# S4 convolution and int4 SwiGLU on one core: later resolvent sums, an earlier load of the shifted kernel, and moved work and loads in the last group

## What is computed

```
x = x + s4(layernorm(x)) + ffn(layernorm(x))

s4:  denom = g[:, None] - Lambda[None, :]            # g: 1024 roots of unity
     cauchy = lambda v: (v[None, :] / denom).sum(-1)
     at_roots = c * (k00 - k01 * (1.0 / (1.0 + k11)) * k10)
     K = ifft(at_roots, L).real                      # L = 1024
     y = irfft(rfft(u, n=2L) * rfft(K, n=2L))[..., :L] + D[0] * u

ffn: Wg, Wu (2752 x 1024), Wd (1024 x 2752): int4, (w - zero) * scale in groups of 64
     h = silu(xn @ Wg.T) * (xn @ Wu.T)
     return h @ Wd.T
```

## Time and profile before

| | us |
|---|---|
| three runs | 1406.25, 1406.70, 1408.76 (median 1406.7) |
| the profiled execution's own time | 1407.06 |
| its span, first to last instruction | 1405.2 |
| TensorE busy (matmuls) | 1318.3 (94%) |
| VectorE busy | 968.1 (69%) |
| GpSimd busy | 682.4 (49%) |
| ScalarE busy | 463.0 (33%) |
| mean granted TensorE clock | 0.976 of 2.4 GHz |

### The profile page before, as it was taken

The page is one execution under the profiler, slowest core; times in us unless marked ns, Lnnn a source line. Parts: engine busy times, 40 slices in busy tenths (PEclk is TensorE's granted clock), DMA queues, the critical chain, the costliest instruction groups (busy, mean ns, idle before and its releaser), DMA issues.

```text
span 1405.2 us, 17059 instructions
## 1 busy us (share of the span) xinstructions
PE 1318.3 (94%) x6302; PEld 625.5 (45%) x6302; DVE 968.1 (69%) x1038; ACT 463.0 (33%) x825; POOL 682.4 (49%) x483
## 2 busy tenths in 40 slices
PE   3688899999999999999999999879999999999998
PEld 2544344344444444444444444334454444444444
DVE  7965799899899989999898988433253433332432
ACT  5744545444544444445454543310000000000000
POOL 6772777777777777879797886610000000000000
PEclk7799999999999999999999999989999999999999
DMA  8111545454555445455545454998345335336331
GB/s 308 32 46 38 166 146 154 126 182 139 161 143 168 133 135 154 147 158 151 163 141 175 128 153 140 381 373 311 113 153 176 98 129 202 99 114 218 98 97 60
DMA packets 165168, 218.09 MB, mean 155 GB/s; under 512 B 42204, under 2 KB 122718, under 8 KB 163166
## 3 DMA queue, kind: packets, MB, share of 16 engines
q1 hardware_dynamic: 164222, 202.79, 46.1%
q10 hardware_dynamic: 864, 14.22, 2.5%
HBM read 139.64 MB, written 77.34 MB: 154 GB/s over the span
## 4 chain that ended last, share of the span: by engine, by line
PE 51%; DVE 2%; SPq 2%; DMA 1%; issue 1%; POOL 1%; ACT 0%; ACTq 0%; DVEq 0%
PE px L1443 15%; PE px L1357 10%; PE pz L1443 8%; PE pv L1470 6%; PE pz L1357 5%; PE py L1443 4%; PE py L1357 2%; DMA kshift<-kpad 1%; SPq L596 1%; DVE wf L1555 1%; DMA w_d<-ds 0%; SPq L600 0%; DVE wf L1527 0%; PE pv L1484 0%; DVE hf L1653 0%
## 5 line engine op out<-in xcount | busy, mean ns | idle before, releaser
L1357 PE MATMUL px<-xo,wo 128*128 128x512 f16 x2016 | 467.4, 386 | 19.2 <-ACT u L986 10.8
L1357 PEld LDWEIGHTS px<-xo,wo 128*128 128x128 f16 x2016 | 198.4, 99 | 264.0 <-issue 28.6
L686 POOL TENSOR_TENSOR wo<-wf,wo 128x512 f16<-128x512 f32 x147 | 239.4, 1638 | 74.9 <-ACT wo L932 74.9
L705 POOL TENSOR_TENSOR hs<-hf,hs 128x512 f16<-128x512 f32 x154 | 211.0, 1376 | 114.9 <-ACT hs L967 114.7
L1443 PE MATMUL px<-wd,hr 128*128 128x512 f16 x1056 | 232.3, 379 | 0.0
L1357 PE MATMUL pz<-xo,wo 128*128 128x512 f16 x1008 | 231.3, 379 | 0.1
L1443 PEld LDWEIGHTS px<-wd,hr 128*128 128x128 f16 x1056 | 102.2, 98 | 118.7
L1357 PEld LDWEIGHTS pz<-xo,wo 128*128 128x128 f16 x1008 | 98.6, 98 | 118.6 <-issue 0.8
L1971 DVE SCALAR_TENSOR_TENSOR acc<-px,acc 128x512 f32<-128x512 f32 x32 | 22.1, 690 | 154.1 <-PE px L1443 126.4
L967 ACT ACTIVATE hs<-hf 128x512 f16<-128x512 f32 x154 | 94.4, 621 | 91.3 <-DVE hf L1619 43.9
L932 ACT ACTIVATE wo<-wf 128x512 f16<-128x512 f32 x147 | 91.4, 623 | 90.0 <-DVE wf L1528 80.7
(11 more groups left out here) (229 smaller groups left out, 1415.0 us busy)
## 6 DMA issues: line engine op xcount, KB each, us to landing
h_d<-hs SPq DMA_DIRECT2D x154, 256.0 KB, 2.4
hr<-h_d SPq DMA_DIRECT2D x56, 704.0 KB, 4.3
w_d<-ds SPq DMA_DIRECT2D x73, 256.0 KB, 2.3
wd<-w_d ACTq DMA_DIRECT2D x4, 2816.0 KB, 15.2
sz<-in_sz_gate SPq DMA_DIRECT2D x21, 512.0 KB, 5.0
sz<-in_sz_up SPq DMA_DIRECT2D x21, 512.0 KB, 4.9
sz<-in_sz_down SPq DMA_DIRECT2D x20, 512.0 KB, 5.3
xc_d<-xo SPq DMA_DIRECT2D x8, 1024.0 KB, 7.7
```

The source lines that it names most:

```text
L686: pool.tensor_tensor(w_dest(t, j, 1), w_place_of(j), w_dest(t, j, 0), ALU.subtract).then_inc(wlo_done, 1)
L705: pool.tensor_tensor(hs[:, j, :, 1, :], h_place_of(p, j), hs[:, j, :, 0, :], ALU.subtract)\
L1357: done = pe.matmul(bank[:, :], wo[t % 2][:, j, wp, k * P:(k + 1) * P], xo[p][:, j, xp, k, :], start=(j in (0, 3) and k == 0 and wp == 0 an ...
```

## The change

1. **Resolvent blocks.** TensorE multiplies block m in unit 8 + 2m, not 7 + 2m. The steps behind it move two units back on VectorE (roots 24, columns 26, rows 28, scale 31) and on TensorE (25, 27, 30). `angle` gets two buffers, and a load waits for the block before the last.
2. **kshift and flip.** `kshift` has a place of its own (over small tables that are done with) and is loaded at the end of group 8, beside unit 32 and after; `flip` is loaded at the start.
3. **Words and scales** have semaphores apart: nibbles wait for words alone.
4. **The short piece's high nibbles** are made by ScalarE (`tail_nibble`), twice 96 rows; VectorE waits for them.
5. **Loads and stores at the change of phase.** The first `acc` are loaded by ScalarE's queue, ahead of `wd3` and `wd4`, once the last `h_second` is done; on SyncE's queue `hr` of product 4 goes ahead of the last seven stores of `h`, and `wd6` behind `hr` of product 5.

The core of the diff (`slab_in` is `words_in` and `scales_in` in the functions left out too, and `angle[m % 2]` stands for `angle`):

```diff
 def slab_arrived(m):
-    return 32 * (m // 2 + 1) + 32 * (m % 2) * ((m >= 63) + (m >= 65))
+    return 16 * (m // 2 + 1) + 16 * (m % 2) * ((m >= 63) + (m >= 65))
...
-        kshift = at("kshift", [P, 2, SB], f32, W0 + 24 * K1)
-        flip = at("flip", [P, P], f32, X0 + 55 * K1)
...
-        angle = small("angle", [P, 2, P])
+        angle = [at(f"angle{i}", [P, 2, P], f32, H0 + i * K1) for i in range(2)]
+        flip = small("flip", [P, P])
+        kshift = at("kshift", [P, 2, SB], f32, place[0])
...
             def load_angle(m):
-                if m > 0:
-                    sp.wait_ge(resolvent_done, m)
+                if m == 0:
+                    sp.wait_ge(xt_done, 56)
+                if m >= 2:
+                    sp.wait_ge(resolvent_done, m - 1)
...
+                if g == 8:
+                    sp.wait_ge(kpad_out, 48)
+                    for n in range(2):
+                        sp.dma_start(kshift[:, n, :], bass.AP(kpad.tensor, n * (P + L // 2) + 1, [[1, P], [1, SB]]))\
+                            .then_inc(kshift_in, 16)
...
             store_h(NG, 0, S4)
-            sp.dma_start(flip[:, :], flip_d).then_inc(flip_in, 16)
-            sp.wait_ge(kpad_out, 48)
-            sp.wait_ge(deq_done, slab_tail(1, 1) + 1)
-            for n in range(2):
-                sp.dma_start(kshift[:, n, :], ...)
             sp.wait_ge(prod_done, PHASE_A)
             load_hr(0, 1, 0)
             load_hr(0, 1, 1)
-            sp.wait_ge(hf_done, 88)
-            load_acc(0, 0)
-            load_acc(0, 1)
             load_hr(0, 2, 0)
...
+            load_hr(0, 4, 0)
+            load_hr(0, 4, 1)
             for j in (A12, A22, A11, S3, S1, S2, S4):
                 store_h(NG, 1, j)
...
+            def tail_nibble(h):
+                m = slab_tail(0, h)
+                slot = m % 2
+                act.wait_ge(words_in[slot], slab_arrived(m))
+                act.wait_ge(wlo_done, 7 * 21 + 3)
+                byte = raw[0:TAIL, slot, :].bitcast(u8).rearrange("p (w b) -> p w b", b=4)[:, :, 0]
+                act.activation(wf[0:TAIL, 0, h, 0, :].bitcast(i32), byte, ACT.Identity, scale=1.0 / 16,
+                               bias=below[0:TAIL, 0:1]).then_inc(nibble_done, 1)
...
             load_wd(2, KC)
-            load_wd(3, KC)
             snap_u3(43)
             silu_second(43)
-            load_wd(4, KC)
             h_high(NG, 1, A12)
             h_high(NG, 1, A22)
+            act.wait_ge(hf_done, 88)
+            for s in range(2):
+                for h in range(2):
+                    act.dma_start(acc[s][:, h, :], x_d[(s + 4 * h) * P:(s + 4 * h + 1) * P, :]).then_inc(acc_in[s], 16)
+            load_wd(3, KC)
+            load_wd(4, KC)
...
-                if n % 2 and 7 <= n < 7 + 2 * M8:
-                    m = (n - 7) // 2
+                if n % 2 == 0 and 8 <= n < 8 + 2 * M8:
+                    m = (n - 8) // 2
...
                 if kh == 0:
-                    dve.tensor_scalar(q[0:TAIL], r[0:TAIL], 4, 15, ALU.arith_shift_right, ALU.bitwise_and)
+                    dve.wait_ge(nibble_done, slab_gate(21) + 2 + h)
                     link(dve.tensor_scalar(q[TAIL:P], r[TAIL:P], 15, None, ALU.bitwise_and))
```

More of the change, by code:

```diff
@@ L287, in s4_plus_int4_swiglu @@
         x_in = [sem(f"x_in{i}") for i in range(8)]
-        slab_in = [sem(f"slab_in{i}") for i in range(2)]
-        ident_in, par_in, tab_in, angle_in, xc_out = (sem(n) for n in ("ident_in", "par_in", "tab_in", "angle_in", "xc_out"))
+        words_in = [sem(f"words_in{i}") for i in range(2)]
+        scales_in = [sem(f"scales_in{i}") for i in range(2)]
+        ident_in, par_in, tab_in, xc_out = (sem(n) for n in ("ident_in", "par_in", "tab_in", "xc_out"))
+        angle_in = [sem(f"angle_in{i}") for i in range(2)]
         stat_done, rstd_done, xn_done, xsum_done, xt_done, xhi_done, xlo_done = \
@@ L379, in load_slab @@
                     sp.wait_ge(deq_done, m - 1)
-                sp.dma_start(raw[:, slot, :], words).then_inc(slab_in[slot], 16)
+                sp.dma_start(raw[:, slot, :], words).then_inc(words_in[slot], 16)
                 sp.dma_start(sz[:, slot, :, :].rearrange("p z w -> p (z w)"),
-                             scales[:, None, :].broadcast_to((16, 8, 1024))).then_inc(slab_in[slot], 16)
+                             scales[:, None, :].broadcast_to((16, 8, 1024))).then_inc(scales_in[slot], 16)
             def load_gate(t):
@@ L451, in _ @@
             sp.dma_start(cs8[:, :, :], small_d).then_inc(tab_in, 16)
+            sp.dma_start(flip[:, :], flip_d).then_inc(flip_in, 16)
             load_down(0, 0)
@@ L618, in _ @@
             load_wd(5, 0, KC)
-            load_hr(0, 4, 0)
-            load_hr(0, 4, 1)
+            load_hr(0, 5, 0)
+            load_hr(0, 5, 1)
             for j in range(7):
@@ L998, in scale_angles @@
                 m = (n - 6) // 2
-                act.wait_ge(angle_in, 16 * (m + 1))
+                act.wait_ge(angle_in[m % 2], 16 * (m // 2 + 1))
                 if m == 0:
@@ L1239, in _ @@
             h_high(NG - 1, 1, A22)
+            tail_nibble(0)
             snap_u3(40)
@@ L1248, in _ @@
             d_high(NG - 1, T2)
+            tail_nibble(1)
             d_high(NG, B11)
@@ L1383, in s4_steps @@
                         .then_inc(cauchy_done, 1)
-                if n == 23:
+                if n == 25:
                     pe.wait_ge(roots_done, 1)
@@ L1389, in s4_steps @@
                         .then_inc(dft_done, 1)
-                if n == 25:
+                if n == 27:
                     pe.wait_ge(kcol_done, 1)
                     pe.transpose(pv[0][0:M8, 0:P], kcol[:, :], ident[:, :]).then_inc(kt_done, 1)
-                if n == 28:
+                if n == 30:
                     pe.wait_ge(kmax_done, 1)
-                    pe.matmul(pv[1][:, 0:M8], angle[0:M8, 0, :], kdiag[:, :], start=True, stop=True).then_inc(kall_done, 1)
+                    pe.matmul(pv[1][:, 0:M8], angle[0][0:M8, 0, :], kdiag[:, :], start=True, stop=True).then_inc(kall_done, 1)
             for b in range(28):
@@ L1775, in kernel_rows @@
                 dve.tensor_copy(krow[:, :, :], rows.rearrange("b (a n) -> b n a", n=2)).then_inc(krow_done, 1)
-                dve.memset(angle[0:M8, 0, :], 1.0)
+                dve.memset(angle[0][0:M8, 0, :], 1.0)
                 dve.tensor_reduce(kend[:, 0:1], rows, AX.X, ALU.max)
@@ L1799, in s4_work @@
                     resolvent((n - 6) // 2)
-                if n == 22:
+                if n == 24:
                     cauchy_sums()
                     roots()
-                if n == 24:
+                if n == 26:
                     kernel_columns()
-                if n == 26:
+                if n == 28:
                     kernel_rows()
-                if n == 29:
+                if n == 31:
                     kernel_scale()
```

25 lines of the change are left out of this document (11 added, 14 removed).

## The result

| | before | changed |
|---|---|---|
| median | 1406.83 us (1406.25 to 1408.76, 4 runs) | 1396.38 us (1395.57 to 1397.65, 4 runs) |
| profiled execution, its span | 1407.06, 1405.2 | 1395.57, 1393.4 |

The ratio is 0.9924, with a 95% interval from 0.9907 to 0.9941: 10.4 us faster, where 28.5 were forecast. The sign was right; the forecast gain was 2.7 times the measured one, and 1396.4 lies above the range of 1370.5 to 1388. To see which terms came, I set the same instruction of both traces side by side: TensorE's `py` product in five units, phase B's first product, and the end of the span.

A forecast was written before the change was run, and what follows sets the result against it. It took TensorE as the bound, busy 1318.3 of 1405.2 us, so only its idle or low-clock stretches could be won. 9.9 + 12.6 + 7.0 - 1.0 = 28.5 us gave 1378.2 us, range 1370.5 to 1388.

The forecast's parts named there:

- Term B: Phase B's start: the early kshift load removes TensorE's 10.17 us wait and the low clock behind it, 12.6 us.
- the second `hr` of product 2: Tight load in phase B: lands at 944.9, TensorE wants it near 945.6, so it only just holds.
- The 1.0 us taken back: Phase B: deducted from the gain because Term C moves the products by 7.0 us but the loads by some 5.5.
- Term A: Phase A: moving the resolvent blocks later removes four TensorE waits for them, 9.9 us, upper bound 16.0.
- the groups: Phase A's groups of four units: 75.2 us each without stalls, where they were 77.8 and 76.6.
- one wait as at unit 9: Roots' sums moved to VectorE's unit 24: costed at nothing, or 1.3 us if the cover is gone.
- the first stall: Unit 9 in phase A: its wait for the resolvent block gives 3.3 us, not 4.4.
- the lower end: Phase A: VectorE slows further as the last stall goes, groups take 77.1 us, Term A is near 5 us.
- rival 3: Phase A: VectorE takes back most of Term A (5 us or less), 1383.1 us and up; chance 0.12.
- Term C: Short piece: ScalarE takes the 96-row shift, the chain is 5 to 6 us earlier, unit 43's wait goes, 7.0 us.
- rival 1: Short piece: the long wait stays since the memset is still there, Term C is 1.3, time 1383.9; chance 0.25.
- the lower bound: Short piece: the remaining 32-row operation inherits the long wait, and only its own 1.3 us go.

The follow-up runs named there:

- e4: Kernel before with only the early kshift and flip loads and the new order of loads and stores on the queues: 1396.29 us, ratio 0.9918.
- e5: Changed kernel with the new order of loads and stores at the change of phase undone, kshift and flip still early: 1405.04 us, ratio 0.9987.
- e1: Changed kernel with the sums at the roots back at VectorE's unit 22, their product still in unit 25: 1391.23 us, ratio 0.9884.
- e11: Kernel of e6, with ScalarE also waiting for wd2 to land before it issues acc: 1387.03 us, ratio 0.9855.
- e10: Kernel of e9, with ScalarE holding acc, wd3 and wd4 until wd2 has landed: 1392.56 us, ratio 0.9892.
- e7: Changed kernel with the roots left in VectorE's unit 24 and TensorE's product with them moved from unit 25 to 26: 1395.00 us, ratio 0.9913.
- e9: Changed kernel with the memset in its place and GpSimd waiting for its end before the next operation: 1400.84 us, six runs from 1392.25 to 1403.09.
- e2: Changed kernel with GpSimd's memset moved from ahead of its run of eight operations to behind it: 1392.24 us, ratio 0.9889.
- e6: Changed kernel with the edits of both e1 and e2 (roots at VectorE's unit 22, memset behind GpSimd's run): 1388.34 us, ratio 0.9865.
- e12: Kernel of e11 with the roots cut in two, the second half ahead of c12 of unit 23: 1389.01 us, ratio 0.9867.

## Why the prediction was right and wrong

- **Term B, right.** 12.6 us were forecast and phase B is 12.9 shorter; in e4, with parts 2 and 5 alone, it is 484.3 us long too. The reading of the queues held: with the old order `hr` takes the place of `kshift` (e5), and the second `hr` of product 2 only just lands in time. What part 5 saves is not issue time: the first `hr` is issued at 909.4 in e5 and at 909.3 in the changed kernel, and lands 23.3 and 10.4 us later. That `hr` landed at 945.3 for 944.9 forecast (the 0.56 MB taken off are 1.3 us at 432 GB/s, not 1.5). The 1.0 us taken back was not needed in the changed kernel, but the margin that it stood for is real: once phase A is faster, TensorE waits there for 0.2 us in e1, 0.45 in e11 and 1.9 in e10.
- **Term A, the step that failed most.** The step was: "no resolvent block is made there, so I cost this at nothing, and if the cover is gone it is one wait as at unit 9, 1.3 us". The sums at the roots were moved to unit 24, where VectorE is latest, with TensorE's step one unit behind: the pattern that the change took away from the resolvent blocks. It cost 5.49 us and 1.28 of clock, 6.8 us and not 0 or 1.3. e7 shows that the distance is not the cause, and e1 that the place is. Of the lead of 10.2 us that the sums had before, 2.8 are gone even at unit 22, where the stalls ahead of it are gone, and 3.2 more in unit 24. I had counted the resolvent block's seven operations, and not these 32, of which six meet GpSimd and take 0.8 to 1.1 us for 0.15.
- **Term A, the groups.** This is a second term that was sized wrong. The short waits for `u` behind each moved block came as forecast (1.3 us, at full clock), and the first stall gave 3.6 us for 3.3 forecast (the 6.5 at unit 24 less the groups). The groups were to be 75.2 us, the old 76.61 less VectorE's wait of 1.41; they are 76.45, and gave 2 x (77.83 - 76.45) + (76.61 - 76.45) = 2.9 us for 6.6. The wait goes, but the same work, now more of it beside GpSimd, is 1.0 us slower. That is the case given as the lower end and as rival 3.
- **Term C, wrong; rival 1 came true.** 7.0 us were forecast on the condition that "the next VectorE operation goes in behind one of GpSimd's", and it did not hold: the next one took 7.14 us. The count of 63 operations in L1525 that never met more than one was no evidence, since none of them stood at this memset. Even the 1.3 us of the lower bound did not come: `c12` of unit 40 starts at 869.58 instead of 869.78, and VectorE then waits 1.75 us for ScalarE's `g` at 878.26 where it had waited 0.97. In unit 43 the wait is 5.58 us for 5.56, and the product behind it takes 4.93 us where it took 4.15. In the other traces with a wait of 5.3 to 6.1 us there it takes 4.2 to 5.3 us, so this 0.8 is scatter as far as is known, and not part 4's.
- **The sum.** -0.1 - 1.0 + 12.9 = 11.8 us by the spans for 28.5. Term B came as forecast, and A and C came to nothing. Rivals 1 and 3 were given, but no case in which term A vanishes whole; with it and rival 1 the sum is 1378.2 + 9.9 + 5.7 = 1393.8, with C at nothing 1395.1.

## What to carry to other kernels

When a wait is removed by moving a consumer later, move through the whole chain behind it and ask of each step what it lands on: a step of many tiny operations in the engine's latest unit can cost more than the wait it replaces. Idle time of an engine that slows beside another is not worth its length; take the group's length with the contention of a group without idle time. And where a load "only just holds", a shift of 1 or 2 us elsewhere can cost 7, as in e9; a wait on what must land first took that back in e10.

## What the runs showed of the hardware

A memset of GpSimd that goes straight into its next operations can keep VectorE out for most of the run: one 32-row operation stood through six of them (7.14 us), and one of 96 rows, which began earlier in the memset, through as many (7.61). All eight traces with the memset there and no stop behind it have it (7.1 or 7.6 us), and the six others do not: with a stop of under 0.1 us behind the memset (e9, e10) the operation took 0.42 us, with the memset elsewhere (e2, e6, e11, e12) 0.90. The Trainium skill (SBUF — State Buffer, "SBUF: two separate sides") gives the pair of ports that VectorE and GpSimd share to whichever starts first, for one whole instruction; the trace agrees where the engines take turns (1.53 and 1.6 us for 0.69 and 1.15), and not here. Why the memset opens such a run was not tried further: the same memset in its later place in e2, at 871.61, goes straight into GpSimd's next operation too, and VectorE's that began inside it took 0.59 us, so a memset is not enough. The second surprise is the tiny operations: 1.12 us for 128 x 8 elements beside GpSimd, 0.15 alone. They end within some 0.02 us of the end of GpSimd's operation (566.58 and 566.56), so their cost is that of the other engine's operation and not of their own size.
